# Block 1's conv by channel groups and its B u behind MoE step 3, two weight splits earlier, GpSimd's residual behind the last split, in a one-core Trainium2 kernel

## The reference, cut to what matters

```python
x = L0_attn_x                       # (1, 4096, 256)
h = _layernorm(x) * (1 + ca) + sa
x = x + ga * _L0_attn_ref(h, ...)   # state space layer, below
h = _layernorm(x) * (1 + cb) + sb
x = x + gb * _L0_ffn_ref(h, ...)    # routed q, k, v (16 experts), attention, routed output

# _L0_attn_ref
proj = layernorm(h) @ W_in;  data, gate = proj[..., :384], proj[..., 384:]
conv = sum(xp[:, j:j + seq, :] * conv_w[:, j] for j in range(3))
u = silu(conv)                                   # conv * sigmoid(conv)
Bu = einsum('bti,si->tbs', u, Bm)                # 16 states
state = state @ M + Bu[t]                        # scan over the tokens
out = sigmoid(gate) * (states @ Cm.T) @ W_out
return h + out
# _L0_ffn_ref: w = routing weights of 16 experts
y = einsum('nc,ech->neh', x, p);  q, k, v = einsum('ne,neh->nh', w, y)   # MoE projections
```

## Time and profile before

| | |
|---|---|
| median of three runs | 1417.59 us |
| the profiled execution's own time | 1418.72 us |
| its span, first to last instruction | 1416.8 us |
| busy: TensorE, its loads | 1373.8 us (97%), 1220.9 us (86%) |
| busy: VectorE, ScalarE, GpSimd | 1153.7 (81%), 675.7 (48%), 706.2 (50%) |
| mean granted clock of TensorE | 0.989 |

### The profile page before, as it was taken

How to read it: one execution, slowest core, us unless ns; L and a number is a source line. 1 busy time by engine, 2 the same in 40 slices (tenths; PEclk the granted TensorE clock), 3 DMA queues, 4 the chain that set the end, 5 groups by cost and what they waited for, 6 DMA issues and landing times. The chain is left out here.

```text
span 1416.8 us, 21192 instructions
## 1 busy us (share of the span) xinstructions
PE 1373.8 (97%) x7050; PEld 1220.9 (86%) x7050; DVE 1153.7 (81%) x2192; ACT 675.7 (48%) x1347; POOL 706.2 (50%) x636
## 2 busy tenths in 40 slices
PE   6989999999999999999999899999999999999997
PEld 5879999999999999999999777878787878878776
DVE  7887786777858768686678698989898999999866
ACT  5611402103022130130101398888888888888983
POOL 2421301313013121130123287888888888989897
PEclk9989999999999999999999899999999999999999
DMA  9101011100111001100138410000001000000000
GB/s 264 42 15 29 20 38 37 31 27 27 40 31 40 28 27 40 31 25 23 53 105 267 148 61 16 16 30 16 31 10 37 8 23 23 16 31 16 10 14 30
DMA packets 83133, 62.96 MB, mean 44 GB/s; under 512 B 13984, under 2 KB 75856, under 8 KB 82768
## 3 DMA queue, kind: packets, MB, share of 16 engines
q1 hardware_dynamic: 54880, 45.94, 10.3%
q10 hardware_dynamic: 28144, 15.67, 3.7%
HBM read 36.55 MB, written 25.03 MB: 43 GB/s over the span
## 5 line engine op out<-in xcount | busy, mean ns | idle before, releaser
L1741 PE MATMUL ps<-w_hi,memory_r 128*128 128x384 f32 x2048 | 565.5, 342 | 0.0
L1442 DVE SCALAR_TENSOR_TENSOR wst<-ps,w_cur,wst 128x384 f32<-128x384 f32 x480 | 295.1, 615 | 164.4 <-PE ps L1741 152.4
L1962 POOL TENSOR_TENSOR memory_rest<-memory_rest,pf 128x512 f32<-128x512 f32 x248 | 345.8, 1394 | 68.5 <-ACT pf L2069 60.4
L1741 PEld LDWEIGHTS ps<-w_hi,memory_r 128*128 128x128 f32 x2048 | 374.9, 189 | 3.4 <-issue 1.4
L1741 PE MATMUL ps<-w_lo,memory_r 128*128 128x384 f32 x1024 | 344.0, 336 | 0.0
L2135 DVE TENSOR_TENSOR p_lo<-pf,p_hi 128x512 fp32r<-128x512 f32 x256 | 282.1, 1102 | 36.0 <-ACT p_hi L2071 35.0
L1741 PEld LDWEIGHTS ps<-w_lo,memory_r 128*128 128x128 f32 x1024 | 193.3, 189 | 4.7 <-issue 1.4
L2069 ACT ACTIVATE pf<-ps 128x512 f32<-128x512 f32 x256 | 153.1, 598 | 72.8 <-PE ps L2241 54.8
L2029 ACT COPY ps<-shift_rows 128x512 f32<-128x512 f32 x254 | 151.7, 597 | 5.8
L2071 ACT ACTIVATE p_hi<-ps 128x512 fp32r<-128x512 f32 x256 | 152.1, 594 | 0.0
L2116 DVE TENSOR_REDUCE mx<-ps 128x1 f32<-128x512 f32 x224 | 147.6, 678 | 1.2 <-PE ps L2230 1.2
(11 more groups left out here) (256 smaller groups left out, 2211.2 us busy)
## 6 DMA issues: line engine op xcount, KB each, us to landing
qk_scratch<-wst ACTq DMA_DIRECT2D x56, 128.0 KB, 2.2
x_scratch<-memory SPq DMA_DIRECT2D x8, 512.0 KB, 2.9
o_scratch<-memory_rest SPq DMA_DIRECT2D x16, 256.0 KB, 3.2
x2b<-x_scratch SPq DMA_DIRECT2D x32, 128.0 KB, 2.2
out_x<-memory_rest SPq DMA_DIRECT2D x32, 128.0 KB, 1.7
v_scratch<-wst ACTq DMA_DIRECT2D x60, 64.0 KB, 1.8
memory<-in_x SPq DMA_DIRECT2D x7, 512.0 KB, 4.0
memory_r<-qk_scratch SPq DMA_DIRECT2D x9, 256.0 KB, 4.6
```

The lines of the kernel that those rows point to most:

```text
L1442: nc.vector.scalar_tensor_tensor(out=dst, in0=src, scalar=w, in1=dst, op0=ALU.mult, op1=ALU.add).then_inc(moe_acc, 1)
L1741: ins = nc.tensor.matmul(ps[:, s % MOE_BANKS, 0:H3], x_part[p][:, k, rows], w_part[:, k, e].rearrange("p t h -> p (t h)"), start=(k == 0 a ...
L1962: nc.gpsimd.tensor_tensor(p_sum[:, p], p_sum[:, p], pf[:, j % PB], ALU.add).then_inc(p_summed, 1)
```

## The change

- `LATE_SPLIT` goes from 8 to 10. VectorE splits expert 8 in front of block 0's first x2 piece and expert 9 behind block 0's last h2 piece; experts 10 to 15 follow steps 0 to 5.
- Block 1's conv, sigmoid and u go by channel groups, with block 0's helpers, which get the block as an argument. Two u stand in front of the routing, the last one behind it. ScalarE takes the three sigmoids in between the gate copies. The counts of `conv_ready` and `u_ready` grow by two in block 1 (`CONV_MORE`).
- `FIRST_BU` goes from 1 to 3, and all three groups of B u stand behind TensorE's step 3.
- GpSimd's low part of x, and with it `residual(0, 1)`, waits for all sixteen splits (`w_lo_ready`, E) and no more for block 1's u.

```diff
-        LATE_SPLIT, FIRST_BU = 8, 1
+        LATE_SPLIT, FIRST_BU = 10, 3
-        CONV_MORE, X2_MORE, DVE_B_MORE = FI - 1, TT - 1, 2 * (TT - 1)
+        CONV_MORE, X2_MORE, DVE_B_MORE = 2 * (FI - 1), TT - 1, 2 * (TT - 1)
...
                 pool.wait_ge(h2t_first, 1)
-                pool.wait_ge(u_ready, FI + 1)
+                pool.wait_ge(w_lo_ready, E)
...
-                def first_sigmoid(f):
+                def first_sigmoid(f, p=0):
 
                     if f == 0:
-                        act.wait_ge(ht_lo_ready, 1)
-                    act.wait_ge(conv_ready, f + 1)
+                        act.wait_ge(ht_lo_ready, p + 1)
+                        wait(act, bu_mm, p)
+                    act.wait_ge(conv_ready, p * FI + f + 1)
...
                 first_squares(2, TT).then_inc(sumsq_ready, 1)
+                first_sigmoid(0, 1)
                 evacuate_projection(FI, FI + 1, 0, 1)
-                evacuate_projection(FI + 1, FI + 2, 0, 1)
+                first_sigmoid(1, 1)
                 act.wait_ge(proj_mm, 4 * FI)
                 nc.scalar.copy(xt_hi[0], first_src).then_inc(h2t_ready, 1)
-                evacuate_projection(FI + 2, 2 * FI, 0, 1)
-                conv_sigmoid(0, 1)
+                first_sigmoid(2, 1)
+                evacuate_projection(FI + 1, 2 * FI, 0, 1)
                 exp(0, 0)
...
                 ins.then_inc(dve_const, 1)
+                split_w(8, 9)
                 more.block(0, 0)
...
                 first_h2(3)
-                for n in range(TAPS - 1):
-                    conv_piece(n, 0, 1)
+                split_w(9, LATE_SPLIT)
+                first_conv(0, 1)
+                first_conv(1, 1)
+                first_u(0, 1)
+                first_conv(2, 1)
                 dve.wait_ge(h2t_ready, 1)
                 tt(xt_lo[0][:, :, 0:P], h2t[:, :, 0:P], xt_hi[0][:, :, 0:P].bitcast(F32), ALU.subtract
                    ).then_inc(xlo_first, 1)
+                first_u(1, 1)
                 for n in range(ROUTE_PIECES - 1):
                     route_piece(n, 0, 0)
-                dve.wait_ge(csig_ready, 1 + FI)
-                tt(sg, sg, cv, ALU.mult).then_inc(u_ready, 1)
+                first_u(2, 1)
...
-                        if is_first(i, p) and s == FIRST_BU + FI - 1:
+                        if is_first(i, p) and s == FIRST_BU:
                             take_input(0, 1, BU_BANK1)
...
-                        if is_first(i, p) and FIRST_BU <= s < FIRST_BU + FI:
-                            if s == FIRST_BU:
-                                pe.wait_ge(proj_evac, 2 * FI + FI + 1)
-                            first_input_term(s - FIRST_BU, 0, 1, BU_BANK1)
+                        if is_first(i, p) and s == FIRST_BU:
+                            pe.wait_ge(proj_evac, 2 * FI + FI + 1)
+                            for f in range(FI):
+                                first_input_term(f, 0, 1, BU_BANK1)
```

More of the change, by code:

```diff
@@ L506, in slot @@
                     if ahead == 1:
-                        sp.wait_ge(u_ready, NB + FI - 1)
+                        sp.wait_ge(u_ready, NB + CONV_MORE)
                         for n in range(3):
@@ L750, in data_out @@
                 def data_out(i, p):
-                    act.wait_ge(conv_ready, past(i, p, 1, 0, CONV_MORE))
-                    act.wait_ge(u_ready, past(i, p, 1, 0, CONV_MORE))
+                    done = upto(i, p, 1, 0) + CONV_MORE if i else FI
+                    act.wait_ge(conv_ready, done)
+                    act.wait_ge(u_ready, done)
                     nc.scalar.copy(data[:, :, 0:TAPS - 1], data[:, :, BT:BT + TAPS - 1]).then_inc(halo_ready, 1)
@@ L969, in slot @@
                         act.wait_ge(w_ready, NB)
-                        act.wait_ge(u_ready, NB + FI - 1)
+                        act.wait_ge(u_ready, NB + CONV_MORE)
                         act.wait_ge(bu_mm, NB)
@@ L1245, in pow_copy, with first_conv @@
                     nc.vector.tensor_copy(powers_t[:, k % 2], ps[:, QK_BANK, P:2 * P]).then_inc(pow_ready, 1)
-                def first_conv(f):
-                    dve.wait_ge(proj_evac, f + 1)
+                def first_conv(f, p=0):
+                    dve.wait_ge(proj_evac, p * 2 * FI + f + 1)
                     for j in range(TAPS - 1):
                         if j:
-                            dve.wait_ge(conv_link, f + 1)
+                            dve.wait_ge(conv_link, p * FI + f + 1)
                         ins = nc.vector.scalar_tensor_tensor(out=cv[:, f], in0=data[:, f, j:j + BT],
@@ L1333, in _, with first_u @@
                 split_w(0, 1)
-                def first_u(f):
-                    dve.wait_ge(csig_ready, f + 1)
+                def first_u(f, p=0):
+                    dve.wait_ge(csig_ready, p * FI + f + 1)
                     tt(sg[:, f], sg[:, f], cv[:, f], ALU.mult).then_inc(u_ready, 1)
@@ L1540, in first_input_term @@
                         pe.wait_ge(late_in, 16 * N_LATE)
-                    pe.wait_ge(u_ready, 1 + f if not p else 1 + FI)
+                    pe.wait_ge(u_ready, p * FI + f + 1)
                     for g in range(NB):
```

## The result

The changed kernel takes 1422.18 us (median of 11 runs, 1418.62 to 1424.05) against 1417.05 us for the kernel before (11 runs, 1415.22 to 1418.02): **5.1 us slower, ratio 1.0037, interval 1.0028 to 1.0046.** That is outside the 0.2% within which I had put most of the chance, and inside the range. The profiled execution of the changed kernel took 1422.18 us, with a span of 1420.4. Against the profiled execution of before (1418.72) that is 3.5 us; the rest of the 5.1 is that the latter stood 1.7 us above its own median of 11 runs.

A forecast was written before the change was run, and what follows sets the result against it. TensorE bounds the kernel, so the change counts through the start of scan step 2 and the clock behind it: -0.8 + 2.25 = +1.4 us on the median 1417.59, forecast 1419.0 us. Range 1416.2 to 1422.7 us.

The forecast's parts named there:

- Rival D: Splits stay near 2.4 us for a reason other than GpSimd; +7, 1424.6 us; chance 0.03.
- The new wait: VectorE reaches the statistics at about 89.9 and stands 9.7 us for the x load, landing at 99.6.
- Rival C: The x load is not the last arrival at the statistics; gain 10 us, 1407.6 us; chance 0.05.
- 0.8 us earlier: The matmul of scan step 2 starts at about 102.9 instead of 103.73, give or take 0.6 us.
- Split 8 costs nothing, covered by the idle 1.49 us: Split 8, 0.95 us at the median, fits VectorE's idle 1.49 us in front of 58.22.
- TensorE stays in front: During VectorE's steps 0 to 5, TensorE keeps ahead, waiting some 2 us behind step 4; step 10 done at about 93.3.
- Behind the statistics: From statistics to scan addition, 2.8 us instead of 3.73, as split 15 (0.95) is gone from between.
- The clock: After 9.6 us of TensorE idle before scan step 2, 4.5 us of low clock follow, costing 2.25 us.
- Rival A: The clock does not fall or is back at once: -0.8, 1416.8 us; chance 0.15.
- The sum: Whole kernel: -0.8 + 2.25 = +1.4 us, forecast 1419.0 us; chance 0.52.
- one rigid train: TensorE's work from scan step 2 at 103.73 on simply follows that moment; busy 76.27 of 76.30 us to 180.
- rival B: Long restart: TensorE at half clock for 11.8 us from scan step 2; +5.1, 1422.7 us; chance 0.25.

The follow-up runs named there:

- experiment 3: Kernel before, with only GpSimd's low part of x waiting for fifteen of sixteen splits instead of block 1's u: 1430.14 us, ratio 1.0096.
- experiment 1: Changed kernel, with GpSimd's low part of x waiting for block 1's last u again instead of the last split: 1416.27 us, ratio 0.9996 to kernel before.
- experiment 5: Changed kernel, with block 2's five layer norm pieces later, at r = 9, 11, 13, 15 and 18: 1413.50 us, ratio 0.9977 to kernel before.
- experiment 6: Changed kernel, with GpSimd waiting for 13 of the 16 splits: 1417.13 us, ratio 1.0001 to kernel before.
- experiment 2: Changed kernel, with 36 unused fill matmuls on TensorE between MoE step 10 and scan step 2: 1419.45 us, ratio 1.0020 to kernel before.
- experiment 4: Changed kernel, with B u spread behind steps 1, 2 and 3 again, one group each: 1421.92 us, ratio 1.0033 to kernel before.
- experiment 9: Changed kernel with later statistics, and GpSimd's residual before its low part of x, both behind the last split: 1412.60 us, ratio 0.9969 to kernel before.
- experiment 10: Changed kernel with later statistics, GpSimd's residual first behind the last split, and VectorE taking B u behind step 2: 1412.27 us, ratio 0.9965 to kernel before.
- experiment 12: Changed kernel, with only VectorE taking B u behind its step 2 instead of step 3: 1419.85 us, ratio 1.0022 to kernel before.
- experiment 8: Kernel before, with only GpSimd behind all sixteen splits and block 2's norm pieces later: 1424.81 us, ratio 1.0054.

## Why the prediction was right on the place and short on the size

- **Bound and mechanism: right.** As forecast, the moment of scan step 2 and the clock behind it decided. The first splits of the slot, 2.35 to 2.59 us before, take 0.94 or 0.95; GpSimd stretches them, since in experiment 3 the same first split of the kernel before takes 0.95 without GpSimd beside it, at the same low clock. Rival D is out.
- **The new wait: right.** VectorE stood 9.72 us at the statistics (9.7 said), GpSimd's three operations and the load added up to 10.9 us behind the last split (90.17 to 101.07), where 10.7 were said. Rival C is out; experiments 1 and 5 take that wait away or nearly so, experiment 6 cuts it to 2.47 us, each in another way, and they win back 5.1 to 8.7 us.
- **"0.8 us earlier" at scan step 2: wrong, it was 0.7 later** (104.41 against 103.73). The statistics started at 101.07 and not at 99.6: the last split ended at 90.17 and not at 88.8, for two reasons. "Split 8 costs nothing, covered by the idle 1.49 us" failed: in this execution GpSimd's low part of x ran from 55.57 and VectorE's second small product of line 1407 ended with it, at 58.06. The idle stretch was eaten, split 8 ran at 57.98, the x2 pieces began 0.63 us later than before, and TensorE stopped 1.39 us at the transposes instead of 0.18. The routing started at 74.20 where 73.66 was said, and VectorE's step 0 at 80.53 and not 80.0. In the profile of experiment 1, with the same code there, the two did not meet and that stop was 0.42. The meeting alone is not due to the change: experiment 3, which has no split 8 there, shows it too (GpSimd from 55.63, the two products 2.17 us) with a stop of 0.55. The cover failed where the meeting and split 8 came together. And "TensorE stays in front" failed for steps 5 and 6: behind its stop for B u it ran at half clock from 87.0 to 90.4, and VectorE waited 0.92 us for it in front of the last split (a second wait of 0.33 came behind that split and delayed nothing of GpSimd's). I had taken the clock for full there.
- **Behind the statistics** two terms were off as well: split 15's absence brought 0.7 us (3.07 from the statistics to the scan addition against 3.73) and not 0.95, and the terms as written give 102.7 for the scan matmul (99.6 + 2.8 + 0.26 from addition to matmul), not 102.9; the two nearly cancel.
- **The clock: 2.25 us forecast, about 3 measured.** The low work is 6.34 us long, where I had taken 4.5; half is 3.2, and the fills of experiment 2 win back 2.7. It lay between the two rows that bounded it. Rival A is out. The Trainium skill's page TensorE: Matmul & The Clock Gate, Part 1, puts the ramp penalty under 1% of a typical kernel's span, and the trace agrees with that figure: 3.2 of 1420.4 us is 0.2%. But to take such a term as nil does not hold here, where it was worth 2.7 of the 5.1 us.
- **The sum.** On the two profiled executions: 0.7 + 3.2 = 3.9, against 3.5 measured; forecast 1.4. On the medians it is 5.1; the 1.6 us between come from the kernel before, whose profiled execution lay 1.7 us above its median of eleven runs. The prediction took all that follows scan step 2 for one rigid train behind it. But low stretches of TensorE stand further back too, at different times in the two executions. Before:

```profile
799.00:810.00 11.00, 8.48 (x20) 0.53 0.90 265
```

and with the change:

```profile
799.00:810.00 11.00, 7.15 (x35) 1.00 0.33 98
530.00:535.00 5.00, 5.00 (x24) 0.66 0.01 2
865.00:869.00 4.00, 4.00 (x15) 0.57 0.12 32
```

  The clock that these stretches lack, times their busy time, is 4.0 us before and 3.4 after, which takes the 3.9 to 3.3. The single runs of one kernel, which differ by 3 to 5 us, go the same way: of the eleven runs of the changed kernel the fastest (1418.62) has a mean clock of 0.995 and the four slowest (1422.84 to 1424.05) 0.990. That speaks against what I put for rival A, three runs of the kernel before within 0.3 us: its eleven spread over 2.8. Why the clock falls in one execution and not in another, no run shows.
- **The range: luck.** 1422.18 lies inside it by 0.5 us, and only because it reached out to rival B. Rival B, the slower one, gave 1422.7 us by a low stretch of 11.8 us that did not occur; the size came from smaller slips of the same sign, 1.5 us at scan step 2 and 1 at the clock, and from what single runs of both kernels scatter. A forecast of +1.4 stood on two large amounts that nearly cancel, some 10 us gained by the splits and given back in the wait for x, each known to 1 us or worse; the chance of slower, 0.28, was too low for that. Rival D's 1424.6 left the clock's term out; with it, its sum is 1427.

## What to carry to other kernels

Before long work is put behind a wait to keep it out of another engine's way, list everything that is queued behind it, down to the transfers that its end releases: here a load with 6.9 us to spare lost 8.2. If it must be late, move its consumer in the written order as well; that one table of steps turned 5 us lost into 3.5 won, and with the residual in front of the low part into 4.6. Keep apart what a stall costs while it lasts and what it costs behind it at half clock.

## What the runs showed of the hardware that I had not expected

- A clean 1.9 us stop of TensorE shortly behind B u was followed by 3.4 us at 0.50 (87.0 to 90.4). The same stands in the profiles of experiments 2, 4, 5 and 9 (stops of 1.85 to 1.89 us), and not where that stop was 0.5 us (experiments 10 and 12). No longer idle stretch stood in front of it from 67 us on. That the stop is the cause rests on these seven executions alone. A forecast that looks for long stops alone misses it, as mine did.
- A GpSimd operation can hold a tiny VectorE one: two products of 128x16 elements (line 1407) took from 55.88 to 58.06, where GpSimd's operation from 55.57 ended at 57.94; in the kernel before the same two were done in 0.25 us at 56.48. It is not the change that makes them meet: of the fourteen profiles ten show it (2.17 to 2.19 us, experiment 3 among them), and four do not (0.25 or 0.26 us: the kernel before and experiments 1, 8 and 9), where GpSimd's operation starts 0.7 us behind the products and not 0.3 in front. These four have a low stretch of TensorE at 48 to 52 us, the ten have none there. The Trainium skill, page SBUF — State Buffer, section "SBUF: two separate sides", calls it an exclusive lock of a shared port pair that is held for a full instruction. The trace agrees: the three stretched splits of the kernel before end at 83.58, 86.62 and 89.65, each 0.8 us behind a GpSimd operation (82.77, 85.79, 88.84), near the 0.95 of a plain split. It goes the other way too: the residual's two operations took 3.07 and 2.87 us beside the splits, and 2.37 and 2.36 with the change, where none ran beside them.
